# Layer entangling matrices multiplied in halves, and spread over the first and the last entry of the attention

## The reference, cut to what matters

```python
h = (jnp.cos(ph) + jnp.sin(ph)) * amp
for l in range(L):                                   # L = 2
    e = h @ ent_w[l] + ent_b[l]                      # ent_w[l]: 256 x 1024
    ent = e @ ent_pw[l] + ent_pb[l]                  # ent_pw[l]: 1024 x 256
    h = _layer_norm(h + ent, ln3_g[l], ln3_b[l])
    t = jnp.einsum('bsd,pdf->pbsf', h, path_w[l]) + path_b[l][:, None, None, :]
    mod = jnp.cos(phase[l]) + jnp.sin(phase[l])
    interf = jnp.sum(t * mod[:, None, None, :], axis=0)
    h = _layer_norm(h + interf, ln4_g[l], ln4_b[l])
```

## Time and profile before

| | us |
|---|---|
| median of 3 runs | 1034.54 (1034.38 to 1035.11) |
| span of the profiled execution | 1033.4 |
| first entry, scores of its pair 0 to scores of the next entry | 28.9 to 91.2 |
| last entry, its pair 0 to the gate products | 218.9 to 299.4 |
| PE busy | 991.0 (96%) |
| DVE busy | 735.9 (71%) |
| ACT busy | 606.6 (59%) |

### The profile page before, as it was taken

One profiled execution on the slowest core, in us unless ns is written; L12 is line 12 of the kernel. 1 busy time (PEld: TensorE's weight loads), 2 busy tenths in 40 slices (PEclk: granted clock), 3 DMA queues, 4 the chain that ended last, 5 costly groups with the idle time before them and its releaser, 6 DMA issues.

```text
span 1033.4 us, 18254 instructions
## 1 busy us (share of the span) xinstructions
PE 991.0 (96%) x6658; PEld 826.1 (80%) x6658; DVE 735.9 (71%) x2003; ACT 606.6 (59%) x1177; POOL 371.4 (36%) x646
## 2 busy tenths in 40 slices
PE   8999999989999898889999999999999999999997
PEld 6555655556658897778989999999999999999997
DVE  6676787767638779866557777766776876677764
ACT  5576657664359774455556666455666655466660
POOL 4455474562131574353722223322222232222600
PEclk9899999998999999999999999999999999999999
DMA  7100010012110001022201010010101011010101
GB/s 249 28 2 22 4 35 8 23 60 85 45 65 4 1 8 36 28 76 62 82 1 42 1 41 4 39 42 1 42 1 42 1 42 42 1 42 1 42 24 59
DMA packets 29234, 36.91 MB, mean 36 GB/s; under 512 B 1780, under 2 KB 26584, under 8 KB 29144
## 3 DMA queue, kind: packets, MB, share of 16 engines
q1 hardware_dynamic: 24728, 31.15, 9.5%
q10 hardware_dynamic: 4416, 4.59, 1.4%
HBM read 31.40 MB, written 4.20 MB: 34 GB/s over the span
## 4 chain that ended last, share of the span: by engine, by line
PE 56%; DVE 4%; POOL 2%; issue 1%; ACT 1%; DVEq 0%; POOLq 0%; ACTq 0%
PE ps L1947 25%; PE ps L1964 24%; PE ps L1837 2%; PE ps L1919 2%; DVE ln_stats L2366 1%; PE ps L1977 1%; PE ps L1888 1%; POOL hs L1734 1%; POOL x_b L1734 0%; PE ps L1851 0%; DVE amp L2402 0%; PE ps L1866 0%; PE ps L1879 0%; PE ps L1788 0%; DVE att L2458 0%
## 5 line engine op out<-in xcount | busy, mean ns | idle before, releaser
L2202 ACT ACTIVATE G<-ps,bias_col 128x512 f32<-128x512 f32 x192 | 135.9, 708 | 176.6 <-PE ps L1947 167.9
L1964 PE MATMUL ps<-w_h,G_h 128*128 128x256 f32 x736 | 204.3, 278 | 0.0
L1964 PE MATMUL ps<-w_l,G_h 128*128 128x256 f32 x736 | 204.0, 277 | 0.0
L1964 PE MATMUL ps<-w_h,G_l 128*128 128x256 f32 x736 | 204.0, 277 | 0.0
L2506 DVE TENSOR_TENSOR G_l<-G,G_h 128x512 fp32r<-128x512 f32 x192 | 155.8, 820 | 59.6 <-ACT G_h L2203 59.6
L1764 POOL TENSOR_TENSOR x_a<-xn,mlp_g 128x1024 f32<-128x1024 f32 x20 | 68.0, 3399 | 333.8 <-DVE xn L2534 333.8
L708 ACT ACTIVATE probs<-ps 128x512 f32<-128x512 f32 (+3 forms) x256 | 98.3, 441 | 96.5 <-PE ps L847 95.7
L1947 PE MATMUL ps<-xT_h,w_h 128*128 128x512 f32 x384 | 151.7, 395 | 0.2 <-issue 0.2
L1947 PE MATMUL ps<-xT_h,w_l 128*128 128x512 f32 x384 | 149.9, 390 | 0.0
L1947 PE MATMUL ps<-xT_l,w_h 128*128 128x512 f32 x384 | 149.5, 389 | 0.0
L1124 DVE CUSTOM_DVE_ANT_0 ps<-ps,q_mask 128x128 f32<-128x128 f32 (+3 forms) x256 | 120.8, 512 | 29.5 <-PE ps L836 29.0
(11 more groups left out here) (330 smaller groups left out, 2099.8 us busy)
## 6 DMA issues: line engine op xcount, KB each, us to landing
w_raw<-L_ffn_W_T SPq DMA_DIRECT2D x12, 1024.0 KB, 5.1
hs<-L_attn_hidden_states SPq DMA_DIRECT2D x8, 512.0 KB, 3.9
x_kept<-hs SPq DMA_DIRECT2D x4, 512.0 KB, 4.1
w_raw<-x_kept SPq DMA_DIRECT2D x2, 1024.0 KB, 5.3
out<-xn SPq DMA_DIRECT2D x3, 512.0 KB, 2.8
w_raw<-L_ffn_ent_w_T SPq DMA_DIRECT2D x1, 1024.0 KB, 9.8
w_raw<-L_ffn_ent_pw SPq DMA_DIRECT2D x1, 1024.0 KB, 12.0
heads_T<-neg_rows SPq DMA_DIRECT2D x64, 2.0 KB
```

The costliest lines, as they stand in the source:

```text
L1964: mm = pe.matmul(ps[:, 4 + t // 2, (t % 2) * D:(t % 2 + 1) * D], x[b % 2][f][:, t * P:(t + 1) * P], w2_chunk(w, f), start=(k == 0), stop=( ...
L2202: act.activation(G32[n % 4], bank, ACT.Gelu, bias=bias)
```

## The change

All entangling and constant products are cut in two halves of 4 matmuls. Layer 0's move to the first entry, layer 1's to pairs 0 to 4 of the last. DVE writes the first half to the result's place and adds the second. The results now lie in `entangled`, a view of `xn[:, 1]`, and `stage_matrix` finds them. The scaling of `stage_c` becomes a generator of its own, `prepare_rows`, at (0,2) and (1,0) of the first entry. Layer 1's weights go over layer 0's into `w2_raw` and `w1_raw`, on SP's queue, at the end of the first entry; ACT's three transfers for them are gone. The fillers are taken out, but for the three at (6,2) of the first entry. `matrix_low` and `matrix_high` now count with two tables, since the matrices are finished in another order.

```diff
-FIRST_AT = ((2, 0, "bias", 0),)
-LAST_AT = ((3, 1, "entangle", (0, 0)), (4, 0, "entangle", (0, 1)), (4, 1, "constant", 0),
-           (4, 2, "entangle", (1, 0)), (5, 0, "entangle", (1, 1)), (5, 1, "constant", 1),
-           (5, 3, "offset", 1), (6, 0, "offset", 3), (6, 1, "offset", 2))
+FIRST_AT = ((0, 3, "entangle", (0, 0, 0)), (1, 2, "entangle", (0, 0, 1)), (2, 0, "bias", 0), (2, 2, "entangle", (0, 1, 0)),
+            (3, 0, "entangle", (0, 1, 1)), (3, 3, "constant", (0, 0)), (5, 2, "constant", (0, 1)))
+LAST_AT = ((0, 1, "entangle", (1, 0, 0)), (0, 3, "entangle", (1, 0, 1)), (1, 1, "entangle", (1, 1, 0)),
+           (2, 1, "entangle", (1, 1, 1)), (3, 1, "constant", (1, 0)), (4, 0, "constant", (1, 1)),
+           (4, 2, "offset", 1), (5, 0, "offset", 3), (5, 2, "offset", 2))
+ROWS_AT = ((0, 2), (1, 0))
+MC_HALF = MC0 // 2
...
-KEEP_AT = {"first": {(0, 3): (4, ("stack", (1, 2))), (2, 2): (3, ("project", (2, 1))), (6, 2): (3, ("project", (3, 2)))},
-           "loop": {},
-           "last": {(0, 3): (4, ("stack", (1, 2))), (1, 1): (4, ("stack", (1, 3)))}}
+KEEP_AT = {"first": {(6, 2): (3, ("project", (3, 2)))},
+           "loop": {}, "last": {}}
...
+    ent_t = g.w2_raw
+    raw_pw = g.w1_raw[:, :, :].rearrange("p c (m d) -> p (c m) d", d=D)
+    entangled = g.xn[:, 1, :, :].rearrange("p (l c) d -> p l c d", c=KC)
...
+                if p == 7 and when == "first":
+                    sp.wait_ge(s["p_work"], WORK.number(i, when, ("constant", (0, 1))))
+                    sp.dma_start(ent_t[:, :, :], A["L0_ffn_ent_w_T"][1].rearrange("(c p) n -> p c n", p=P)
+                                 ).then_inc(s["ent_in"], 16)
+                    sp.dma_start(raw_pw, A["L0_ffn_ent_pw"][1].rearrange("(c p) n -> p c n", p=P)
+                                 ).then_inc(s["ent_in"], 16)
...
-        ent_dram = A["L0_ffn_ent_w_T"][1].rearrange("(c p) n -> p c n", p=P)
-        raw_loads += [(g.xn[:, 1, :, :], ent_dram[:, 0:4, :], "ent_in"), (x_in, ent_dram[:, 4:8, :], "ent_in"),
-                      (raw_pw1, A["L0_ffn_ent_pw"][1].rearrange("(c p) n -> p c n", p=P), "ent_in")]
...
-                for m in range(MC0):
+                for n in range(MC_HALF):
+                    m = part * MC_HALF + n
...
-                    mm = pe.matmul(work[:, 0:D], lhsT, raw_pw[l][:, m, :], start=(m == 0), stop=(m == MC0 - 1))
+                    mm = pe.matmul(work[:, 0:D], lhsT, raw_pw[:, m, :], start=(n == 0), stop=(n == MC_HALF - 1))
...
-                l, c = arg
-                chain.settle()
-                v.tensor_copy(raw_path[:, 2 * l + 1, c, :], work[:, 0:D]).then_inc(s["work_read"], 1)
-                if c:
-                    v.wait_ge(s["work_read"], WORK.number(i, when, (kind, arg)) + 1)
-                    add_identity(2 * l + 1)
+                l, c, part = arg
+                tile = entangled[:, l, c, :]
+                if part == 0:
+                    v.tensor_copy(tile, work[:, 0:D]).then_inc(s["work_read"], 1)
+                else:
+                    v.wait_ge(s["work_read"], WORK.number(i, when, (kind, (l, c, 0))) + 1)
+                    v.tensor_tensor(tile, tile, work[:, 0:D], ALU.add).then_inc(s["work_read"], 1)
+                    if c:
+                        v.wait_ge(s["work_read"], WORK.number(i, when, (kind, arg)) + 1)
+                        add_identity(entangled[:, l, :, :])
...
-        PREPARE_AT = ((1, 2), (1, 3), (2, 0), (2, 1), (2, 2), (2, 3), (3, 2), (3, 3), (4, 0), (5, 1), (5, 3), (6, 1),
-                      (6, 3))
+        PREPARE_AT = ((1, 2), (1, 3), (2, 0), (2, 2), (2, 3), (3, 2), (3, 3), (5, 1), (5, 3), (6, 1), (6, 3))
```

More of the change, by code:

```diff
@@ L921, in use_work @@
             elif kind in ("entangle", "constant"):
-                l = arg[0] if kind == "entangle" else arg
+                l, part = arg[0], arg[-1]
                 if l:
-                    pe.wait_ge(s["ent_in"], 48)
+                    pe.wait_ge(s["ent_in"], 32)
                 else:
@@ L1178, in take_work @@
             elif kind == "entangle":
-                l, c = arg
-                chain.settle()
-                v.tensor_copy(raw_path[:, 2 * l + 1, c, :], work[:, 0:D]).then_inc(s["work_read"], 1)
-                if c:
-                    v.wait_ge(s["work_read"], WORK.number(i, when, (kind, arg)) + 1)
-                    add_identity(2 * l + 1)
-            elif kind == "constant":
-                chain.settle()
-                v.wait_ge(s["wave_rows_in"], 32)
-                v.tensor_tensor(g.stage_c[:, 2 * arg + 1, :], work[:, 0:D], ent_pb[:, arg, :], ALU.add
-                                ).then_inc(s["work_read"], 1)
+                l, c, part = arg
[8 more added lines that the diff above has]
+                        add_identity(entangled[:, l, :, :])
+            elif kind == "constant":
+                l, part = arg
+                row = g.stage_c[:, 2 * l + 1, :]
+                if part == 0:
+                    chain.settle()
+                    v.tensor_tensor(row, work[:, 0:D], ent_pb[:, l, :], ALU.add).then_inc(s["work_read"], 1)
+                else:
+                    v.wait_ge(s["work_read"], WORK.number(i, when, (kind, (l, 0))) + 1)
+                    v.tensor_tensor(row, row, work[:, 0:D], ALU.add).then_inc(s["work_read"], 1)
             elif kind == "offset":
@@ L1238, in prepare @@
             chain.settle()
-            add_identity(0)
-            add_identity(2)
+            add_identity(raw_path[:, 0, :, :])
+            add_identity(raw_path[:, 2, :, :])
             yield
@@ L1247, in prepare, with prepare_rows @@
             yield
+            for st in SPLIT_NUMBER:
+                matrix_low(st)
+                yield
+        def prepare_rows():
+            v.wait_ge(s["mod_in"], 16)
             v.wait_ge(s["wave_rows_in"], 32)
@@ L1255, in prepare @@
             yield
-            for st in MATRIX_NUMBER:
-                matrix_low(st)
-                yield
         def normalise(i, when):
@@ L1275, in entry @@
             norm = iter(())
-            work_ahead = prepare()
+            work_ahead = prepare() if when == "last" else prepare_rows()
             for n, (p, r) in enumerate(slots):
@@ L1294, in entry @@
                 kind, arg = table.get((p, r), (None, None))
-                if when == "last" and (p, r) in PREPARE_AT:
+                if when == "last" and (p, r) in PREPARE_AT or when == "first" and (p, r) in ROWS_AT:
                     next(work_ahead)
@@ L1639, in _ @@
     def _(sp):
-        sp.wait_ge(first["p_work"], WORK.number(B - 1, "last", ("constant", 1)))
+        sp.wait_ge(first["p_work"], WORK.number(B - 1, "last", ("constant", (1, 1))))
         sp.dma_start(last_g, A["L0_ffn_ln4_g"][1:2, :].broadcast_to([P, D])).then_inc(rows_in, 16)
@@ L1695, in _ @@
     def _(pool):
-        pool.wait_ge(first["p_work"], WORK.number(B - 1, "last", ("constant", 1)))
+        pool.wait_ge(first["p_work"], WORK.number(B - 1, "last", ("constant", (1, 1))))
         pool.memset(sel.bitcast(F32), 0.0).then_inc(wave["g_zero"], 1)
```

30 lines of the change are left out of this document (15 added, 15 removed).

## The result

| | before | changed |
|---|---|---|
| median of the runs | 1034.9 us (5 runs, 1034.38 to 1035.22) | 1039.15 us (5 runs, 1036.39 to 1040.47) |
| ratio to before | | 1.0040, 95% interval 1.0028 to 1.0053 |
| span of the profiled execution | 1033.4 us | 1038.7 us |

The changed kernel is 4.2 us slower in the medians and 5.3 us in the two profiled spans. The forecast was 1033.5 with a range to 1038.0, so both the centre and the range missed. The profiled execution of the changed kernel is the longest of its five (1040.47 us); the shortest, 1036.39 us, had a mean granted clock of 0.987 where the other four had 0.982 or 0.983.

What follows compares the result with a forecast made beforehand. PE, busy 96% of a 1033.4 us span, was taken to bound the kernel. First entry +7.9, border +5.5 and last entry -14.4 gave -1.0, so a median of 1033.5 us, range 1028.5 to 1038.0.

Steps and rivals of the forecast that it cites:

- First entry: First entry: six added product halves, less covered idle time and fillers, plus some DVE time: +7.9 us, bounds 7.0 to 9.5.
- The border: Start of the second entry: `x_in` queued behind two 1 MB loads makes PE wait: +5.5 us, bounds 2.5 to 9.
- the wait: Second entry's turning of x: PE stands still until `x_in` lands behind the two loads, 4.9 us.
- the clock: Behind the standstill at the border: PE is granted half clock for a stretch, adding 1.7 us.
- the recovered waits: Steps behind the turning: ACT and DVE have caught up, so PE's waits for them go, -1.1 us.
- Last entry: Last entry: six products go, four halves and moved offsets come, in three parts: -14.4 us, bounds -17 to -11.
- the middle: Last entry, 246.3 to 287.1: six products go, DVE becomes the later engine, 26.5 us where 40.8 stood: -14.3.
- the tail: Last entry behind 287.1: two offsets, 2.0 us, leave a stretch where PE is busy 10.6 of 12.3 us: -1.6.
- The prediction's own sign: Last entry: if it takes over 69 us, the second half of the forecast's sum is wrong.
- the first part of the last entry: Last entry up to 246.3: four halves come, waits and two fillers go: +1.5 us, bounds -1 to +3.
- the second rival: Border: loads at 268 GB/s, wait 6.3, low clock 3.0, border 8.8 in all; slower at 1038.2 us, chance 0.14.
- the third (DVE sets the pace): Last entry: DVE sets the pace from pair 2 on, the gain is only 10; 1037.9 us, chance 0.09.

Runs made afterwards that it cites:

- e4: Changed kernel with layer 1's two 1 MB loads issued at the same point by ACT on its own queue; 1035.95 us, ratio 1.0002.
- e1: Changed kernel with layer 1's two 1 MB loads moved behind `x_in`, into pairs 2 and 4 of the second entry; 1030.82 us, ratio 0.9957.
- e5: e1 plus two fillers each at (4,1), (5,1) and (5,3) of the last entry; 1029.88 us, ratio 0.9948.
- e8: e1 with DVE's four splits of the stage matrices moved later in the last entry; 1029.21 us, ratio 0.9941.
- e6: e1 plus three fillers at (5,2) of the second and third entry; 1030.70 us, ratio 0.9949.
- e7: e1 with the fillers of both e5 and e6; 1029.56 us, ratio 0.9939.
- e9: e8 plus the three fillers at (5,2) of each middle entry; 1028.35 us, ratio 0.9935.
- e10: Changed kernel with only DVE's four splits moved later in the last entry, loads still ahead of `x_in`; 1035.91 us, ratio 1.0009.
- e2: e1 with the last entry's three offsets put back at (5,3), (6,0) and (6,1); 1034.55 us, ratio 0.9994.
- e3: Kernel before with two 1 MB loads that nothing needs added ahead of `x_in` at the first entry's end; 1041.83 us, ratio 1.0059.

## Why the prediction was wrong

**First entry: right.** Forecast +7.9, measured +8.0. The sum came, its parts less so. Five halves came within 0.4 us of what they were put at, the one at (0,3), where filler and idle time stood, among them. At (1,2), where nothing was idle and 1.85 was put, that step and the next grew by 2.6, since PE now waits for DVE ahead of the half:

```profile
39.15 1.99 PE L946 MATMUL ps<-w_raw 128*128 128x256 f32 x8
41.07 0.50 PE L856 MATMUL ps<-heads_T 64*128 64x512 f32 x2
...
46.39 1.99 PE L946 MATMUL ps<-w_raw 128*128 128x256 f32 x8 [0.78 <-DVE x_l L1172]
```

The first takes 1.92 us from its start to the next scores, where 1.62 stood. The wait of 0.78 is the part of DVE's that the prediction let return to PE as 0.5, without a place. DVE did 47.6 us of work instead of 43.3, and was still idle for nearly 23 us.

**The border: mechanism right, the clock's part undersized.** Forecast +5.5, measured +6.8. Both kernels can be cut from the first scores of the second entry to those of its pair (2,0):

```profile
99.12:120.65 21.53, 15.65 (x114) 9.91 (x114) 10.55 (x40) 12.51 (x32) 7.66 (x22) 0.84 0.33 115
```

```profile
91.23:105.98 14.75, 13.47 (x114) 8.25 (x113) 10.89 (x41) 12.60 (x32) 7.64 (x22) 1.00 0.09 31
```

The first is of the changed kernel, the second of the one before; both hold the same 114 matmuls. The step put the wait at 4.9 (5.34 came), the clock at 1.7 (PE's busy time grew by 15.65 - 13.47 = 2.2) and the recovered waits at 1.1 (idle time apart from the wait for x fell from 1.28 to 0.54, so 0.7). All three terms erred by 0.4 or 0.5 to the same side. The prediction's own 307 GB/s gave 5.3, and it went below that for its row of single loads. Within the wait two things cancelled. The loads moved faster than 307 GB/s, but SP issues `x_in` 1.1 us later, behind the two issues (96.95 to 98.06), which the step did not count; that 5.3 came so near is in part luck.

The Trainium skill (DMA: Bandwidth & Descriptors, Queues, rings and completion order) has the descriptors of one issuer's queue consumed in ring order on each DMA engine, and the engines serving several queues in turn. The changed kernel agrees with the first: the loads landed at 102.4 and 106.3 and `x_in`, behind them in the queue, at 107.7. The second no run here bears out or refutes: beside the loads on another queue (e4) `x_in` took 7.1 us and landed with the last of them, against 4.0 in e1 without them.

**A short stretch at the lower clock in the second entry: not foreseen.** +1.5. Pair 6 took 9.40 us where 7.87 stood before, at 0.50 from 154.0 to 157.4. The third entry had the same in the kernel before and has it in the changed one. It was there in e1, e5 and e8, too, which have no stall at the border, so it isn't the stall's. What brought it into the second entry is open. PE waits for DVE's maxima for 0.94 us ahead of it in both kernels, and with that wait covered it was in none of the three profiles (e6, e7, e9); in the kernel before, that wait alone had not brought it about.

**Last entry: -14.4 forecast, -11.0 measured; this is the step that failed.** By its parts, cut at the scores of (3,1) and (6,0): the first +0.1, the middle -13.1, the tail +2.0, where it had +1.5, -14.3 and -1.6. The first came out better since two stretches at half clock that the kernel before had there, the second of the earlier trace rows and the one in which the filler of the earlier trace rows took 2.05 us, were gone. The middle was right within its bounds, DVE being the later engine as said: 22.6 us busy of 25.7, four waits of PE. The term that broke is the tail. The step took the two offsets off a stretch in which PE is busy for 10.6 of 12.3 us, at the full clock as the rows of before had it, and never asked what clock the tail would run at once the six products were gone from pairs 3 to 5. The waits for DVE ahead of it had been priced as idle time only. In e8, where the tail ran at 1.00, it took 11.1 us (-1.8, forecast -1.6), the middle 24.9 (-13.9), and the whole entry was 64.9 us instead of the 66 forecast. So without the long stretch the last entry gives 15.6, more than forecast; the stretch costs some 4. The prediction's own sign, a last entry over 69 us, came with 69.5, but of the 3.4 us that the entry missed only 1.2 are the middle, where it expected the trouble.

**The sum.** From -1.0 to the measured +5.3 it is 6.3 us: 3.6 for the tail, 1.5 for the short stretch, 1.3 for the border, 1.2 for the middle and 0.1 for the first entry, less 1.4 for the first part of the last entry (rounded). With the border at 6.8 and a tail at the full clock the forecast's sum would have been near nothing, 7.9 + 6.8 - 14.4 = +0.3, and 1.5 slower with the short stretch. The prediction named the clock as what decides in the first part of the last entry, and in the second rival; at the end of that entry it did not look for it. The second rival, with 1038.2 the nearest to what came, had the border at 8.8 for a reason that did not hold, since the loads didn't crawl at 268 GB/s; the third (DVE sets the pace) named the engine whose splits, moved, made the long stretch rarer; but it had DVE's pace as the loss, and that was 1.2 us of it.

## What to carry to other kernels

Before a large load is put into a queue, look at what stands behind it there and when that is needed: the same 2 MB cost 6.7 us ahead of a 512 KB transfer with 1.5 us of slack, and nothing that shows when issued 15 and 30 us behind it, between two pairs' rows. Another queue at about the same point was no way out (e4, 5.1 us above e1), since a row of 2 KB and the 512 KB were late there as well. When solid PE work is taken out of a stretch that another engine paces, price what follows it at the half clock too, not only the idle time; moving a few small steps of that other engine, which removed a wait of 0.70, was worth 3.2 us (e10 to the changed kernel) and 1.6 us (e8 to e1, not clear of noise). Where runs of one kernel fall into groups, look at the mean clock of each run before a median is explained, since one profile shows only one of the groups.

## What the runs showed of the hardware

The loads at the border moved more than the rows that the prediction had chosen. In the changed kernel:

```profile
102.00:104.00 2.00, 0.48 (x9) 0.14 (x1) 0.80 (x5) 0.99 (x5) 1.23 (x3) 1.00 1.09 383
```

383 GB/s over 2 us, against 307 in the earlier trace rows. The trace of the kernel before had such a stretch as well, at the program's start, where it loads its first weights: 386 GB/s over the 4 us from 12. The prediction did not look there. The figure of about 358 GB/s per core that the Trainium skill gives (DMA: Bandwidth & Descriptors, Specifications), as half of a stack's 716, was no ceiling for this core, with no other core running the kernel; the measurement decides here.

A stretch at half clock lasted 13.7 us in the last entry of five kernels (the changed one, e1, e2, e4, e6), with PE busy for 13.85 of 14.00 us in e6. What started and ended it, beyond that DVE's splits in a later place made it rarer, is open; which part of the change brought it in (the products gone from pairs 3 to 5, the fillers gone, DVE's added work) no run takes apart. A 2 KB transfer made PE wait 2.18 us beside 2 MB that stood in another engine's queue (e4), and another one 1.31 us beside 1 MB (e3).
